# A mixture-of-experts and state-space block on one core: another order of the same steps in the four kinds of slots

## What is computed

```
x = x + 0.5 * ffn(layernorm(x))          # 8 experts of 128 -> 512 -> 128, silu, the 2 best by softmax
x = x + attn(layernorm(x))
x = x + 0.5 * ffn(layernorm(x))          # the same weights

attn(x):   x1 = x + mamba(rmsnorm(x));  o = mamba(rmsnorm(x1))
           return x1 + o + 0.1 * reads(o) @ w_read.T       # chunked linear memory with decay
mamba(x):  xm, res = split(x @ in_w.T + in_b)              # 256 channels each
           xm = silu(conv4(xm) + conv_b);  x_dbl = xm @ xp_w.T
           delta = softplus(x_dbl[:64] @ dt_w.T + dt_b);  B, C = x_dbl[64:80], x_dbl[80:96]
           h[t] = h[t-1] * exp(delta[t] * A) + delta[t] * xm[t] * B[t]     # 16 states per channel
           y = sum over states(h * C) + xm * D
           return (y * silu(res)) @ out_w.T + out_b
```

## Time and profile before

| | us |
|---|---|
| median of 3 runs | 1679.26 (1675.97 to 1679.89) |
| the profiled execution | 1679.97 |
| its span in the profile | 1678.1 |
| first slot begins, last slot ends | 86.7, 1604.0 |
| one steady round, from 662.9 to 854.1 | 191.2 |

### The profile page before, as it was taken

How to read it: one execution, slowest core, us unless ns; L and a number is a source line. 1 busy time by engine, 2 the same in 40 slices (tenths; PEclk the granted TensorE clock), 3 DMA queues, 4 the chain that set the end, 5 groups by cost and what they waited for, 6 DMA issues and landing times. The chain is left out here.

```text
span 1678.1 us, 29290 instructions
## 1 busy us (share of the span) xinstructions
PE 1327.8 (79%) x8754; PEld 1191.0 (71%) x8754; DVE 1391.7 (83%) x2149; ACT 1278.2 (76%) x2660; POOL 650.4 (39%) x681
## 2 busy tenths in 40 slices
PE   7978567878888787888878788877878787668778
PEld 6867456767777686777767687776867676457668
DVE  3367989989899888989889898989899888978742
ACT  3489658978788788979889797978889698548722
...
GB/s 198 110 88 141 79 81 153 144 169 133 157 133 136 147 140 177 144 162 122 143 152 137 163 140 178 142 160 115 146 162 130 165 145 104 82 137 106 156 90 45
DMA packets 144231, 227.04 MB, mean 135 GB/s; under 512 B 13648, under 2 KB 79440, under 8 KB 143952
## 3 DMA queue, kind: packets, MB, share of 16 engines
...
...
## 5 line engine op out<-in xcount | busy, mean ns | idle before, releaser
L977 ACT ACTIVATE dA<-delta,A 128x255 f32<-128x255 f32 x1024 | 425.7, 495 | 5.3 <-DVE hs L1345 4.4
L1351 DVE TENSOR_TENSOR_SCAN hs<-dA,b_r 128x512 f32<-128x512 f32 x256 | 297.6, 1202 | 17.2 <-PE b_r L664 12.3
L1345 DVE TENSOR_TENSOR_SCAN hs<-dA,dbu 128x1024 f32<-128x1024 f32 x128 | 292.7, 2287 | 16.6 <-ACT dA L977 10.2
L539 PE MATMUL b_h<-xsT,wst 128*128 128x128 f32 x1680 | 253.7, 299 | 35.4 <-issue 28.6
L539 PEld LDWEIGHTS b_h<-xsT,wst 128*128 128x128 f32 x1680 | 227.2, 209 | 55.3 <-issue 53.4
L1363 DVE TENSOR_TENSOR G<-hs,b_r 128x1024 f32<-128x1024 f32 x192 | 233.3, 1215 | 33.1 <-PE b_r L675 27.6
L551 PE MATMUL b_out<-w2s,hT 128*128 x1680 | 234.8, 286 | 11.0 <-ACT ys L898 9.2
L847 ACT ACT_TABLE_LOAD x182 | 233.5, 1283 | 3.9 <-PEq L1751 0.7
L551 PEld LDWEIGHTS b_out<-w2s,hT 128*128 128x128 f32 x1680 | 215.8, 200 | 16.3 <-issue 14.8
L664 PE MATMUL b_r<-prm,scaled 128*128 128x128 f32 x1024 | 173.6, 300 | 57.0 <-ACT scaled L993 28.8
L993 ACT ACTIVATE scaled<-duT,dtT 128x256 f32<-128x256 f32 x512 | 217.0, 500 | 1.4 <-PE b_r L664 1.1
...
## 6 DMA issues: line engine op xcount, KB each, us to landing
...
```

Of the source, the lines that this page charges most:

```text
L539: last = mm(H[r % 2][:, w], wst[k % NW][:, w], xsT[i // CH % 2][:, t:t + P], start=True, stop=True)
L977: last = do(dA[j % 4][:, d, k, 1:], delta[b][:, k, 1:], ACT.Exp, scale=A[:, k, s:s + 1])
L1345: V.tensor_tensor_scan(flat(hs[j % 2]), flat(dA[j % 4]), flat(dbu[n % 2]), 0.0, ALU.mult, ALU.add)\
L1351: V.tensor_tensor_scan(hs[j % 2][:, d, :, :].rearrange("p h t -> p (h t)"), dA[j % 4][:, d, :, :].rearrange("p h t -> p (h t)"), R[u % 2][ ...
```

## The change

The strings in `ORDER` are replaced. Every engine gets the same steps in each kind of slot, in another order, but for two things that cross a border between slots: of TensorE's 35 pieces, 13 now stand in A and 22 in B (16 and 19 before), 16 in C and 19 in D (18 and 17 before), and ACT's `F9` stands at the end of A, not at the start of B. The rest of the kernel is the same text. Since table loads follow from the order, ACT's own sequence changes in them too: 5, 9, 5 and 5 loads in A, B, C and D of a steady round become 5, 9, 7 and 7.

```diff
--- before.py
+++ after.py
@@ -109,28 +109,37 @@
 
 ORDER = {
     "tensor": (
-        "p1 t0 k0 t1 in t2 p2 k1 t3 p1 t4 p1 k2 xp p1 t5 dt p1 t6 k3 p1 t7 m1 k4 t8 p1 dx p2 m2 k5 t9 p2 t10 m3 t11 k6 p2 m4 k7 p1",
-        "t0 p1 t1 t2 p2 k0 p1 t3 p2 fturn k1 t4 t5 fgate p3 fcount p2 k2 p3 out t6 k3 p5 t7 turn t8 k4 in k5 t9 k6 t10 xp t11 dt k7 dx",
-        "t0 p1 t1 p1 t2 p1 k0 t3 p3 k1 out p1 t4 p1 k2 t5 p1 t6 p1 turn t7 k3 in k4 t8 p1 xp t9 t10 dt k5 p1 t11 p3 k6 p1 dx p2 k7",
-        "t0 t1 p3 t2 k0 p2 t3 p2 fturn p2 fgate k1 p1 t4 fcount t5 p2 turng k2 p1 in k3 t6 p4 k4 t7 t8 xp dt k5 t9 t10 m1 t11 dx k6 m2 m3 k7 m4",
+        "t0 t1 p1 in t2 k0 p2 k1 t3 t4 p2 t5 k2 xp dt p1 t6 k3 t7 m1 p1 t8 dx p1 k4 m2 p1 k5 p1 t9 p2 k6 p1 "
+        "t10 t11 m3 m4 k7",
+        "p1 t0 t1 k0 t2 p4 t3 p2 fturn p1 fgate t4 p1 k1 fcount k2 p3 t5 p1 out p2 k3 t6 p6 k4 p1 t7 turn t8 "
+        "in k5 t9 t10 xp dt t11 k6 k7 dx",
+        "p2 t0 t1 t2 p2 k0 p1 out t3 k1 p3 t4 p1 k2 p1 t5 t6 t7 turn k3 in k4 t8 p1 t9 xp t10 dt k5 p3 k6 p1 "
+        "t11 p1 dx k7",
+        "p3 t0 p1 t1 p1 t2 k0 p2 t3 p2 fturn p1 fgate t4 t5 k1 fcount p1 k2 p2 turng p1 in p1 t6 k3 p4 k4 t7 "
+        "xp t8 dt t9 k5 t10 m1 t11 dx k6 m2 m3 k7 m4",
     ),
     "scalar": (
-        "d0 e1 d1 d2 F0 e3 d3 F1 F2 e5 F3 r xm d4 proj d5 sp F4 F5 e7 F6 oT dx F7 d6 d7 v F8 rT",
-        "F9 e1 d0 d1 F10 F11 F12 e3 F13 d2 F14 F15 fxT d3 F16 F17 d4 F18 F19 d5 d6 F20 F21 e5 ftanh F22 F23 e7 F24 turned r xm d7 proj sp dx",
-        "d0 e1 F0 d1 F1 F2 e3 F3 e5 F4 d2 d3 d4 d5 d6 turned d7 e7 F5 F6 r xm F7 proj F8 sp F9 F10 F11 dx",
-        "e1 F12 F13 d0 d1 F14 F15 e3 F16 F17 F18 fxT e5 F19 d2 d3 turned d4 F20 F21 ftanh F22 F23 r xm F24 d5 proj e7 sp d6 oT dx v d7 rT",
+        "e1 d0 d1 d2 F0 e3 d3 e5 F1 F2 r F3 xm d4 proj d5 sp F4 oT e7 F5 dx d6 F6 F7 v d7 F8 rT F9",
+        "d0 e1 d1 d2 F10 F11 F12 F13 e3 F14 fxT d3 ftanh F15 d4 F16 F17 F18 d5 d6 F19 F20 F21 F22 e5 F23 F24 "
+        "e7 turned r xm d7 proj sp dx",
+        "F0 d0 e1 d1 F1 d2 F2 d3 F3 e3 F4 e5 d4 e7 d5 turned d6 d7 F5 F6 F7 r xm F8 proj sp F9 F10 F11 dx",
+        "e1 F12 F13 d0 d1 F14 F15 e3 F16 F17 F18 fxT d2 e5 d3 F19 turned F20 d4 F21 r F22 F23 xm F24 ftanh d5 "
+        "e7 proj sp d6 oT dx d7 v rT",
     ),
     "vector": (
-        "b0 s0 g0 s1 gate g1 b2 s2 g2 s3 low b4 g3 delta s4 g4 s5 b6 mask g5 s6 g6 s7 xb g7",
-        "b0 fstats s0 s1 g0 fnorm b2 s2 flog ftop g1 fplace gate g2 s3 b4 xsum g3 un s4 g4 s5 g5 b6 fweights s6 g6 low s7 delta g7 fsum",
-        "b0 s0 s1 g0 gate b2 g1 xsum s2 s3 un g2 b4 lx g3 s4 s5 g4 ln b6 low s6 g5 unx delta g6 s7 g7",
-        "b0 fstats s0 s1 fnorm b2 g0 flog ftop g1 fplace s2 g2 s3 gate g3 b4 s4 fweights g4 s5 low g5 b6 delta s6 mask g6 s7 g7 xb fsum",
+        "b0 s0 s1 g0 gate b2 g1 s2 g2 s3 b4 low g3 delta s4 g4 s5 mask g5 b6 s6 g6 s7 xb g7",
+        "b0 s0 fstats s1 g0 fnorm b2 s2 flog ftop g1 fplace gate g2 s3 xsum g3 b4 un s4 g4 fweights s5 b6 g5 "
+        "s6 low s7 g6 delta g7 fsum",
+        "b0 s0 gate g0 s1 b2 g1 xsum s2 s3 un g2 b4 s4 lx g3 s5 g4 b6 ln low s6 g5 unx delta g6 s7 g7",
+        "b0 fstats s0 s1 fnorm g0 b2 flog ftop g1 fplace s2 g2 gate s3 b4 g3 s4 g4 s5 b6 fweights low g5 "
+        "delta s6 mask g6 s7 g7 xb fsum",
     ),
     "gpsimd": (
-        "skip a2 a3 a4 a5 a6 a7",
-        "froot skip sc0 sc1 sc2 a2 sc3 sc4 fkeep rms a3 sc5 sc6 sc7 rs a4 ga0 ga1 ga2 ga3 a5 ga4 ga5 ga6 ga7 a6 a7",
-        "skip rms rs a2 a3 lnx rmsx a4 a5 a6 a7",
-        "froot skip sc0 sc1 sc2 a2 sc3 sc4 fkeep a3 sc5 sc6 sc7 a4 ga0 ga1 ga2 ga3 a5 ga4 ga5 ga6 ga7 a6 a7",
+        "a2 skip a3 a4 a5 a6 a7",
+        "froot skip sc0 sc1 sc2 sc3 sc4 rms a2 rs a3 sc5 sc6 a4 ga0 sc7 ga1 ga2 ga3 a5 fkeep ga4 ga5 ga6 ga7 "
+        "a6 a7",
+        "rms rs skip a2 a3 lnx rmsx a4 a5 a6 a7",
+        "froot skip sc0 sc1 a2 sc2 sc3 sc4 sc5 sc6 a3 a4 sc7 ga0 ga1 ga2 ga3 ga4 ga5 ga6 ga7 a5 fkeep a6 a7",
     ),
 }
```

## The result

| | before | after |
|---|---|---|
| median of 4 runs, on the same chip | 1677.7 us | 1750.5 us (1746.9 to 1757.1) |
| ratio | 1 | 1.0438 (95% interval 1.0414 to 1.0462) |
| span of the profiled execution | 1678.1 us | 1748.3 us |
| A, B, C, D, mean of rounds 2 to 6 | 39.6, 54.9, 42.2, 54.1 | 38.5, 59.3, 45.6, 57.4 |
| a round | 190.8 us | 200.7 us |

The change makes the kernel 4.4% slower, 73 us. The forecast was 1666 us, its range ended at 1702. The lengths of slots are taken, as before, from one `b0` on DVE to the next. A became 1.1 us shorter; B became 4.4 us longer, C 3.4 and D 3.3. One execution of a later run, cd_repair2, took 4393 us for no cause on record, and its ratio leaves that one out.

The account below looks back on a forecast made before the run. DVE works 171.4 of a 191.2 us round, with B and D ending in GpSimd's gathers. A -1.5, B +1.6, C -0.3, D -1.8 make -2.0 us a round, times 7 -14: 1680 to 1666 us, range 1640 to 1702.

Parts of the forecast that it names:

- a chain over GpSimd: Slots B and D: length set by fplace, GpSimd's queue, landing of the gathers, then fsum; fplace to fsum 34.8 us in B.
- no wait at C's `gate`: Slot C: gate at +3.6 instead of +6.9 needs a7 of B landed; bounds 0 and +3.3 us; a wait would refute.
- `F24` in B at +33.5: Slot B, ScalarE: the last results leave 1.1 us later than before, when F24 ended at +32.4.
- The sum over ScalarE's queue up to `F19`: Slot B: from fxT's end at +10.6, step durations and table loads add up to +27.2.
- DVE reaches `b6` at +36.1 and `fsum` at +52.1: Slot B: DVE waits 4.9 us at b6 for t9, then has 11.1 us of steps queued before fsum.
- the cover of "nothing to 2.5 us": Slot B: DVE's long wait stays hidden behind gathers coming at +51.9 to +54.6; past the cover each us counts.
- rival 3: Slot B: late F24 holds ga0, deciding from +39.6; DVE's cover used up; B +4, 1700 us in all; chance 0.22.
- C at -0.3: Slot C: -0.6 us for fewer hand-overs against 0 to +3.3 for a7's landing; taken as -0.3 us.
- ACT has 4.1 us of air here: Slot C: ScalarE's idle time, set against the two more table loads there.
- D at -1.8, with `mask` at +43.9: Slot D: s5 at +32.8, mask at +43.9, fsum at about +49.3; -1.8 us (bounds -3.3 and 0).
- e7: Slot D, ScalarE step of 1.6 us class e: stands before proj, so t9 behind dt comes at +36.4.
- Rival 4: Slots C and D: added table loads lie on the path, 2.6 us in each; 1702 us in all; chance 0.06.

Follow-up runs that it names:

- cd_repair2: cd_new with 12 unread matmuls ahead of t6 in C and, in D, proj one step earlier and t9 ahead of dt; 1697.4 us, ratio 1.0115.
- mix2: Kernel before with m4 behind m3 in A, one piece between fturn and fgate in D, a5 and fkeep behind gathers in B and D; 1660.0 us.
- cd_new: Kernel before with the changed orders of all four engines in slots C and D alone; 1714.8 us, ratio 1.0233.
- f19_late: Kernel before with one turn of ScalarE's slot B from the change, F19 behind d5 and d6; 1704.3 us, ratio 1.0151.
- loads: Kernel before with two more table loads ahead of d3 in C and two ahead of d4 in D each round; 1699.7 us, ratio 1.0135.
- warm_all: Changed kernel with unread matmuls added on TensorE ahead of t6 in C, fcount in B and D, and dt in D; 1756.5 us, ratio 1.0449.
- d_turns: Changed kernel with two turns of D taken back: proj one step earlier on ScalarE, t8 xp t9 dt on TensorE; 1747.4 us, ratio 1.0437.
- fewer_loads: Changed kernel with ScalarE's steps reordered in C and D for one pair of table loads less in each; 1768.9 us, ratio 1.0548.
- cd_repair: cd_new with t0 ahead of pieces in C and D, 12 unread matmuls ahead of t6 in C, proj earlier and t9 before dt in D; 1719.6 us.
- the two halves: Kernel before with the changed orders in A and B alone, 1701.2 us, and in C and D alone, 1714.8 us.

## Why the prediction was wrong, step by step

**Right.** The reading that B and D of the kernel before end in a chain over GpSimd: mix2 takes from it what was reckoned for B. In the changed kernel: A's wait at `xb` is gone (38.5 us, -1.1 for a forecast of -1.5). `fplace` in B at +17.2 (+17.1), the logits in D at +10.6 (+11.0), D's gathers landed at +49.6 to +50.9 (+48.6), 212 loads of 1.28 us, a wait at `b6` in B of 5.1 us (4.9), no wait at C's `gate`. That last bound was near, though: in cd_new, where B is shorter, `gate` does wait 0.7 us for the landing.

**Wrong: `F24` in B at +33.5.** It ended at +36.6. The sum over ScalarE's queue up to `F19` gave +27.2; it was +28.8, because it had only durations and no waits (0.5 at `F13`, 0.7 at `F17`). The next link, from the end of `F19` to that of `F24`, was 6.3 us and measured 7.8. The sum took six pieces at 0.95 to 1.05 us, as in the earlier trace rows, one directly behind the other; in four of five rounds the link took 7.5 to 7.7 us at the full clock, with `U14` waiting 0.4 to 0.7 us, and in the fourth round 8.5, with `U13` and `D12` at the lower one. f19_late shows, in the old kernel, what `F19`'s late place is worth.

**Wrong: DVE reaches `b6` at +36.1 and `fsum` at +52.1.** The size of the wait was right, its place was not. DVE came to `b6` at +39.0, since `g4`, three steps ahead, was given no wait; `k4` on TensorE stands behind six late pieces and cost 2.3 us there in the mean. DVE was at `fsum` at +55.9, level with the gathers, and the cover of "nothing to 2.5 us" was gone. What rival 3 named is what happened in B: `ga0` at +39.9, past its point of +39.6, DVE's cover used up, and B +4.4 for a price of +4. It had 0.22, and it had D and A still winning.

**Wrong: C at -0.3.** It was +3.4. The clock is missing from the forecast of C altogether, though the earlier trace rows showed 0.91 there. The kernel before also idles ahead of `in` (2.3 us at `t6`), but a piece, `D2`, stood between that and `in` and took the slow stretch. The change moves `D2` ahead of the wait, and `in`, on which the next slot's start depends, takes its place. The term "ACT has 4.1 us of air here" was wrong as a method: air belongs to a place in a queue, 1.0 us at the old `d3`, and loads shows 2.2 us lost there with two loads. Whether the loads cost anything where the change has them is not shown: its `d3` has 7.2 us of air. And C's first `t0` stands behind two pieces, for which C's `b0` waits 1.0 us as soon as B is late. The sign named beforehand, a wait at C's `gate`, did not come.

**Wrong: D at -1.8, with `mask` at +43.9.** It was +3.3 and +49.1. The forecast asked what is late next, and named the right steps, but walked them again by durations: no wait at `b4` (1.2), `g4` (1.1) and `s5` (which began at +36.2, not +32.8: `F23`, with `d5` behind it, began at +30.7, 2.4 us later than before), then `dt` behind `proj` behind `e7`, 2.7 us of idle TensorE, and `m1` to `m4` in part at the lower clock. The forecast counted the piece taken from between `fturn` and `fgate` as a gain and did not look at `fcount`, ahead of which the change leaves no piece either: TensorE waits 1.22 us there and runs slow behind it, which warm_all shows to be 1.7 us at `s5`. d_turns and cd_repair2 show that the order of `proj`, `e7`, `t9` and `dt` is 2.6 to 2.9 us of D. The two are not a sum: cd_repair2 has the old length with `s5` still at +36.3. By its own sign, "if D keeps its length because `d5` or `mask` come no sooner", the prediction named this failure. Rival 4, loads on D's path, was wrong (fewer_loads); for C it is open.

**The chances.** Slower had 0.28, and its two cases ended at 1702, since each slot's failure was priced by itself, with the other slots still winning. They failed together: each slot was given its gain with all engines arriving as early as before, and the clock, named for B alone, was at work in C and D.

**Open.** In D, `F23` waits until +30.7 for `U14`, whose matmuls in the record end at +29.2; in the kernel before, and in warm_all at +28.9, the two follow each other at once. So the wait goes with the slow stretch, but why the record has the matmuls end earlier is not known, and no run has the filling ahead of `fcount` alone. C keeps 1.1 us in cd_repair that neither the clock nor `t0` explains. B's 4.4 us were not won back by any run. The last 13 us of the whole, beyond the two halves, were seen but not taken apart.
